# Attention with projections in its gaps: VectorE's order, TensorE's order and the slots of eight query tiles

## The reference

```python
q = x @ Wq.T;  k, v = (heads of) context @ Wk.T, context @ Wv.T   # 32 heads of 16
q = _rmsnorm(q);  k = _rmsnorm(k)
attn = jax.nn.softmax(einsum('bhnd,bhmd->bhnm', q, k) * HEAD_DIM ** -0.5, axis=-1)
x = x + tanh(g_xattn[1]) * einsum('bhnm,bhmd->bhnd', attn, v)     # x in q is layernorm(x)
x = x + tanh(g_ffn[1]) * L1_ffn(layernorm(x))    # best of 64 slices by sign scores, spline on 8 values
```

## Time and profile before

| | us |
|---|---|
| median of 3 runs (1193.0 to 1193.74) | 1193.59 |
| the profiled execution | 1199.1 |
| its span, first to last instruction | 1197.3 |
| attention stage, first score of group 0 to last evacuation | 305 |
| TensorE busy over the span | 996.9 (83%) |
| VectorE busy | 705.4 (59%) |
| ScalarE busy | 671.7 (56%) |
| GpSimd busy | 507.9 (42%) |

### The profile page before, as it was taken

One profiled execution on the slowest core, in us unless ns is written; L12 is line 12 of the kernel. 1 busy time (PEld: TensorE's weight loads), 2 busy tenths in 40 slices (PEclk: granted clock), 3 DMA queues, 4 the chain that ended last, 5 costly groups with the idle time before them and its releaser, 6 DMA issues. The chain is left out here.

```text
span 1197.3 us, 27953 instructions
## 1 busy us (share of the span) xinstructions
PE 996.9 (83%) x9515; PEld 569.6 (48%) x9516; DVE 705.4 (59%) x1724; ACT 671.7 (56%) x1090; POOL 507.9 (42%) x442
## 2 busy tenths in 40 slices
PE   5789989968899888899999999935899887988850
PEld 2455655456677555577777777722122211211120
DVE  8676754578887456322223222216476788787687
ACT  5565645454454257444445444425678867899950
POOL 1132331256676264455556555521232354343522
PEclk9899999989999989899999999977799989999965
DMA  6543231489993596667676766655777856687311
GB/s 239 174 133 118 81 134 56 155 197 198 229 212 111 180 334 144 131 120 117 115 145 117 120 115 116 114 111 146 148 152 161 173 135 159 131 177 136 71 41 63
DMA packets 183493, 170.87 MB, mean 143 GB/s; under 512 B 137172, under 2 KB 138772, under 8 KB 182484
## 3 DMA queue, kind: packets, MB, share of 16 engines
q1 hardware_dynamic: 155554, 111.62, 36.5%
q0 software_dynamic: 25888, 56.43, 24.5%
q10 hardware_dynamic: 1954, 1.54, 0.4%
HBM read 80.82 MB, written 65.20 MB: 122 GB/s over the span
## 5 line engine op out<-in xcount | busy, mean ns | idle before, releaser
L2012 ACT ACTIVATE sb_atp<-ps_atpS 128x1024 f32<-128x1024 f32 x256 | 243.2, 1036 | 48.6 <-PE ps_atpS L1754 48.6
L1445 PEld LDWEIGHTS ps_shpH<-sb_roxT,sb_rowt 128*128 (+1 forms) x2844 | 170.0, 107 | 20.7 <-DVE sb_roxT L1312 1.8
L1445 PE MATMUL ps_shpH<-sb_roxT,sb_rowt 128*128 128x128 f16 (+1 forms) x2844 | 174.4, 221 | 1.6 <-DVE sb_roxT L1312 1.6
L1434 PE MATMUL ps_shpY<-sb_rowt,sb_rohhl 128*128 (+1 forms) x711 | 171.3, 387 | 4.7 <-DVE sb_rowt L1325 4.3
L1766 PE MATMUL ps_atpO<-sb_atp,sb_atv 128*17 128x512 f32 x1024 | 139.6, 618 | 30.9 <-ACT sb_atp L2012 20.8
L1069 POOL DMA_INDIRECT sb_roxg<-xn,sb_roentry x79 | 86.1, 1090 | 96.6 <-DMA sb_roentry<-list 75.3
L1168 ACT ACTIVATE sb_roh<-ps_shpH,sb_rob 128x128 f32<-128x128 f32 (+1 forms) x237 | 68.9, 362 | 103.6 <-PE ps_shpH L1445 100.4
L1434 PEld LDWEIGHTS ps_shpY<-sb_rowt,sb_rohhl 128*128 128x128 f16 (+1 forms) x711 | 67.6, 99 | 73.7 <-issue 10.4
L1157 ACT ACTIVATE sb_roy<-ps_shpY,sb_roentry 128x512 f32<-128x512 f32 x79 | 54.2, 686 | 81.3 <-PE ps_shpY L1434 77.7
L1057 POOL DMA_INDIRECT list<-sb_shentry,sb_shposb x64 | 73.2, 1144 | 34.4 <-DVE sb_shposb L1240 19.2
L1312 DVE COPY sb_roxT<-ps_shpR 128x1024 f16<-128x1024 f16 x40 | 27.6, 690 | 94.9 <-PE ps_shpR L279 94.9
(11 more groups left out here) (355 smaller groups left out, 1771.7 us busy)
## 6 DMA issues: line engine op xcount, KB each, us to landing
sb_rowt<-rw SPq DMA_DIRECT2D x15, 768.0 KB, 9.7
sb_rowt<-rw SPq DMA_DIRECT2D x15, 704.0 KB, 6.8
kst<-sb_kykp SPq DMA_DIRECT2D x16, 512.0 KB, 3.0
qst<-sb_quqp SPq DMA_DIRECT2D x12, 512.0 KB, 3.9
vst<-sb_kyvt SPq DMA_DIRECT2D x16, 272.0 KB, 2.5
sb_atv<-vst SPq DMA_DIRECT2D x32, 136.0 KB, 3.4
sb_stage<-ctxT SPq DMA_DIRECT2D x4, 1024.0 KB, 6.2
sb_shxin<-x SPq DMA_DIRECT2D x16, 256.0 KB, 10.6
```

Source lines behind the costliest of these rows:

```text
L1434: last = e.matmul(pY[it.p][:, :], hhl[it.p][0:n, x, k * P:(k + 1) * P], weight(value, 2 * W1 + w + k * D, n, D), start=j == 0, stop=j == l ...
L1445: last = e.matmul(rpH[it.p][0:n, f * P:(f + 1) * P], weight(ex["up"], w + k * FF + f * P, P, n), rxT[it.p][:, x + k, :], start=j % (3 * KD ...
L2012: S.done(e.activation(pr[n % 6][:, :], pS[n % 3][:, :], ACT.Exp, scale=HD ** -0.5 / SA ** 2), "atexp")
```

## The change

Three edits, all in `phase_back`. No instruction is added or removed; the order changes on TensorE and VectorE, and the slots of tiles 8 to 15, and with them of their pairs, change on all engines.

```diff
-        q_slot = [-16, -15, -14, -13, -4, -2, 0, 2, 6, 8, 12, 14, 20, 22, 30, 32]
+        q_slot = [-16, -15, -14, -13, -4, -2, 0, 2, 4, 6, 8, 10, 12, 14, 26, 30]
@@ TensorE, in group it
                         scores(it, 2 * m + 1)
+                        if m == 0 and it.n - 1 in started:
+                            project(started[it.n - 1], 6, 12)
                         if m > 0:
                             weigh(it, m - 1)
                         elif it.n > 0:
                             weigh(it.back(1), 3)
-                        if m == 0 and it.n - 1 in started:
-                            project(started[it.n - 1], 6, 12)
@@ VectorE, in slot h
                 for it in q_at(h, 2):
                     norm(it)
+                for it in g_at(h, 3):
+                    normalise(it)
+                for it in q_at(h, 6, FIRST):
+                    projected(it)
+                for it in g_at(h, 2):
+                    evacuate(it)
                 for it in n_at(h, 1):
                     scale(it)
                 for it in n_at(h, 2):
@@
                 for it in q_at(h, 3, FIRST):
                     low(it)
-                for it in g_at(h, 2):
-                    evacuate(it)
-                for it in q_at(h, 6, FIRST):
-                    projected(it)
-                for it in g_at(h, 3):
-                    normalise(it)
                 for it in q_at(h, 7):
                     squares(it)
```

## The result

| | before | after |
|---|---|---|
| median, 20 runs each (us) | 1195.51 | 1189.6 |
| ratio after to before, 95% interval | | 0.995 [0.9935, 0.9965] |
| profiled execution (its span) | 1199.1 (1197.3) | 1187.84 (1186.0) |
| attention stage, first score to last evacuation | 305.0 | 301.3 |

The change saves 5.9 us; 15.0 were forecast. The two profiled spans differ by 11.3 us, but 7.4 of it lies before the stage (the first score of group 0 starts at 833.63, not at 840.99), where nothing was changed. What can be compared between single profiles is the stage. Its group 0 alone varied from 12.3 to 14.6 us over the profiles of this study, always with half a projection in it, so that the table of the experiments counts groups 1 to 31: 291.11 before, 287.66 after, 3.5 less. The tail is 51.3 before and 51.1 after. The forecast stage, with the 1.7 taken off, was 290.0 us; it took 301.3, 11.3 more.

What follows compares the result with a forecast made beforehand. Took ScalarE's exponentials to bound groups without projection, TensorE full groups, VectorE's queue groups 12 and 16. 112.2 + 92.0 + 84.1 = 288.3, 16.7 under 305.0; less 1.7 leaves 15.0: 1193.6 - 15.0 = 1178.6 us, range 1171 to 1190.

Steps and rivals of the forecast that it cites:

- the 1.7 taken off: Whole stage: 1.7 us deducted from the saving for VectorE instructions lengthened beside GpSimd's y, bounds 0 and 7.
- The reading of before: Groups 12 and 16: VectorE's queue delays normalise and sb_o; group 12's 3.9 us wait and slow clock should go.
- 1.1 us stay, and I add 0.8 for what follows at slots 24 and 38.: Groups 11 to 21: ScalarE's remaining wait for law at slot 22, 1.1 us, plus 0.8 us where roots and statistics meet.
- The wait goes: 9.88 - 0.34 = 9.5.: Full groups: first weighted values no longer wait 0.34 us for the raw copy, so 9.88 becomes 9.5 us.
- TensorE hardly stops: TensorE bounds it: Full groups before the change: TensorE is the bound, at 9.88 us a group.
- The stalls of the dense stretch: Groups 1 to 9: VectorE lateness costs 0.9 us in each of groups 4, 6, 8, and 1.1 us at slot 18.
- The other sum: Dense stretch: with every pair's low in its long form, stalls are 1.3 us each, not 0.9; 1.2 us more in all.
- Half groups: Groups 15 to 18, half a projection each: 15 and 17 at 8.48 us, 16 and 18 at 9.0; 35.0 together.
- full groups in a row cost TensorE time that single halves hide: Groups 0 to 10: 112.2 us, 0.9 more than now, since single halves hide TensorE time under ScalarE.
- The transposed tiles: Rival, dense stretch: low and its transpose come late for projections; at 8.5 us the time is 1199; chance 0.08 (slower).
- It does not do what it says: Rival, groups 12 and 16: collision handed to parts, casts and law, 14.2 us of excess stay; 1192.8; chance 0.04.
- VectorE bound: Rival, dense stretch: VectorE bounds all nine full groups, 10.9 us each, 8.6 more than the sum; 1187; chance 0.18.

Runs made afterwards that it cites:

- the cast short: Kernel after the change, with GpSimd's cast of the query parts for tiles 12 to 15 cut to 64 columns a tile; ratio to before 0.9942.
- law early and the stores late: Kernel after, with VectorE's scales and spread2 right behind evacuate, and SyncE's y store two slots and pair's store one slot later; ratio to before 0.9896.
- law early: Kernel after, with VectorE's scales and spread2 (second layernorm) moved right behind evacuate; ratio to before 1.0023.
- the stores': Kernel after, with SyncE's y store two slots later and the pair's store one slot later, behind the keys; ratio to before 0.9958.
- TensorE's order: Kernel before, with only TensorE's edit: a projection's second half ahead of the last weighted values; ratio to before 1.0040.
- the pair's store behind the keys: Kernel after with scales and spread2 moved up on VectorE, plus SyncE's store to qst of tiles 8 to 15 behind the slot's keys; ratio to before 1.0026.

## Why the prediction came out wrong

**The reading of before held.** Sb_o's wait and the clock behind it were a cost in groups 12 and 16, the change does free sb_o (10.4 us of waits to 1.1), group 16, which has no roots in it any more, takes 8.95 for a forecast of 9.0, group 10 8.96 for 9.0, groups 22 to 31 83.7 for 84.1, and the tail only shifts.

**The step that failed: "1.1 us stay, and I add 0.8 for what follows at slots 24 and 38."** It priced law's lateness in the eleven groups 11 to 21 at 1.9 us. Groups 11 to 14 and 19 to 21 took 65.3 instead of 57.0, so this term is 8.3 us short. Two errors are in it.

First, the wait itself: 2.51 and 2.56 us instead of 1.9 in all, 3.2 more. The subtraction (4.1 less what no longer stands ahead of law) was right: with the cast short, 0.99 us of wait are left at group 12 where 1.1 was worked out. What it missed is contention, which was weighed, but only for `low`. Before, low stood between the scaling and law and took the long form itself (1.50 at 964.13), while the cast ended ahead of law:

```profile
962.66 2.42 POOL L1902 CAST sb_quqp<-sb_quqn 128x1024 f16<-128x1024 f32 x2 [0.19 <-DVE sb_quqn L2148]
...
966.75 0.21 DVE L2200 SCALAR_TENSOR_TENSOR sb_laab<-sb_lars,sb_gate,sb_lamv 128x1 f32<-128x1 f32 x1
966.88 0.74 DVE L2201 SCALAR_TENSOR_TENSOR sb_law<-sb_law,sb_lars,sb_labs 128x512 f32<-128x512 f32 x1
```

With spread and low gone from that slot, the instructions that make law start beside the cast and lose the 1.5 us instead: 0.87 and 1.60 where these rows have 0.21 and 0.74.

Second, its price: a microsecond of ScalarE's wait was counted as one of the group. These groups have no projection, so ScalarE bounds them and hides no wait of its own; TensorE's idle then costs the slow clock too, and ScalarE waits again for the late scores (1.54 us in group 12). The slow clock was priced for sb_o and forgotten for law. The waits of 2.51 and 2.56 cost 3.9 and 5.3 us over the 8.17 of an undisturbed group, 4.2 more than themselves. The last 0.9 is group 21 (8.57 for 7.66). With law early and the stores late groups 12 and 20 take 8.2 and 8.7.

**What the prediction did not have at all** is the limiter behind law, SyncE's queue. It is named once in the working ("behind which SyncE's queries and keys for later groups stand"), but for the pair's store, not for y's, and in the kernel after it costs little, since law is late first. Mending law alone did not bring the forecast (law early).

**"The wait goes: 9.88 - 0.34 = 9.5."** The wait went and the group stayed: 9.84, 3.1 us in nine groups. TensorE in a full group after, to be held against the earlier trace rows:

```profile
857.54 0.61 PE L1754 MATMUL ps_atpS<-sb_atq,sb_atk 64*128 64x512 f16 x4
...
861.00 1.05 PE L1766 MATMUL ps_atpO<-sb_atp,sb_atv 128*17 128x512 f32 x8
...
862.89 1.05 PE L1766 MATMUL ps_atpO<-sb_atp,sb_atv 128*17 128x512 f32 x8 [0.29 <-ACT sb_atp L2012]
```

The next weighted values start 5.35 us into the group now and 5.39 before: they wait for an exponential that starts 3.36 us into the group in both kernels, once its scores are made. "TensorE hardly stops: TensorE bounds it" missed the 0.3 us in which ScalarE bounds it.

**The stalls of the dense stretch** were sized nearly right: 11.00 for groups 4, 6 and 8 is 1.16 over the undisturbed 9.84 where 0.9 stood, group 9 has 0.87 where 1.1 stood, group 1 an unforeseen 0.43. VectorE in group 4, its start at 877.22:

```profile
877.78 1.50 DVE L2111 TENSOR_TENSOR sb_quxhl<-sb_quxs,sb_quxhl 128x512 f16<-128x512 f32 x1
...
881.37 0.68 DVE L2116 COPY sb_quraw<-ps_atpO 128x512 f32<-128x512 f32 x1
```

The raw copy starts 4.15 us into the group (4.0 to 4.8 was worked out), with a low in its long form ahead of it. The other sum, 1.3 each with every pair's low in its long form, was nearer than 0.9: the low of groups 4, 6 and 8 takes 1.50 each time. The 1.7 taken off for such instructions elsewhere is not seen as a term of its own.

**Half groups** 15 and 17 take 9.06 and 9.41, not the 8.48 of group 19; 1.4 us in four groups. A first half costs all of its 1.40 us on top of 7.66, and more in 17. Group 19 before held a second half only; 16 and 18, which hold second halves, came out at the forecast's 9.0. So the sentence that full groups in a row cost TensorE time that single halves hide was wrong also: apart (1.4 and 0.8) or together (9.84 - 7.66), the halves cost about 2.2 us a tile.

**The rivals.** VectorE is not the bound of the dense stretch (every second group is 9.84). The transposed tiles are not late: TensorE waits once, 2.0 us, for sb_quxT in the whole stage. "It does not do what it says" had the mechanism, the collision handed on to parts, casts and law, and 14.2 us as its price: of that excess 9.2 are there (12.11 + 13.46 - 2 x 8.17), at groups 12 and 20. The cases were not exclusive: the forecast's waits went, and the rival's came, for a gain between the two. That 1189.6 falls between the 1184 and 1191 of "VectorE bound" is luck: its mechanism, nine slower full groups, isn't there.

The 3.5 us of the windows and the 5.9 of the medians [4.2 to 7.8 by the interval] leave 2 us without a place; one profile of each kernel can't say more.

## What to carry to other kernels

When a wait is removed, look for the next one on the same instruction and on the others in that window, and price it with the slow clock behind it: here sb_o hid law, law early in its turn laid open SyncE's queue, the raw copy hid an exponential, and law's place and the stores' were worth +2.7 and -0.9 us alone and -7.6 together. Before moving urgent work to the head of an in-order queue, list all pieces of that window which another engine waits for, not just the one with the longest wait, and look at what each will run beside once its neighbours are gone. Here a store that waited for a slow engine was better placed behind the loads of later work. An edit that is harmless in company (TensorE's order) can cost 4.8 us alone, so test parts both alone and by leaving them out.

## What the runs showed of the hardware

A VectorE instruction on 128x1 took 0.87 us instead of 0.28, and one on 128x512 1.60 instead of 0.74, beside two GpSimd casts that took 2.41 us together; before, with the casts over, they took 0.21 and 0.74. After 3.4 us of idle TensorE's eight matmuls took 1.91 us at a granted clock of 0.50; with the short cast they took 1.38 after 1.86 us of idle in group 12 and 1.05 after 1.66 us in group 20; undisturbed 1.05. A transposing DMA of queries, issued in a burst, was there after 6.9 us with law early and after 11.0 with the pair's store behind the keys, with DMA shares of 0.96 to 1.32 in the windows that they crossed.
